# Query and key chunks of 128 different columns, and random features of head pairs as 32-row products in four row tiles

## The reference, cut to what matters

```python
qkv = (x @ W_qkv).reshape(b, n, 3, H, DH)            # H = 12 heads, DH = 16
q, k, v = (qkv[0], qkv[1], qkv[2])                   # after a transpose
def _phi(t, random_features):                        # M = 64 random features
    norm_sq = 0.5 * jnp.sum(t * t, axis=-1, keepdims=True)
    proj = jnp.einsum('bhnd,md->bhnm', t, random_features)
    return jnp.exp(proj - norm_sq) * (1.0 / math.sqrt(M))
q_p = _phi(q, random_features)
k_p = _phi(k, random_features)
kv = jnp.einsum('bhnm,bhnd->bhmd', k_p, v)
out = jnp.einsum('bhnm,bhmd->bhnd', q_p, kv)
normalizer = jnp.einsum('bhnm,bhm->bhn', q_p, jnp.sum(k_p, axis=2))[..., None]
out = out / (normalizer + 1e-06)
```

## Time and profile before

| what | value |
| --- | --- |
| median of 3 runs | 511.91 us (508.93 to 514.75) |
| span of the profiled execution | 511.0 us |
| TensorE busy | 424.5 us (83%), 2630 instructions |
| TensorE weight loads busy | 298.8 us (58%) |
| VectorE busy | 307.6 us (60%) |
| ScalarE busy | 227.5 us (45%) |
| GpSimd busy | 159.0 us (31%) |
| mean granted clock of TensorE | 0.883 of full speed |
| attention's features stage, first L750 to first L809 | 18.3, 17.2, 15.5 and 15.4 us in groups 0 to 3 |

### The profile page before, as it was taken

One profiled execution on the slowest core, in us unless ns is written; L12 is line 12 of the kernel. 1 busy time (PEld: TensorE's weight loads), 2 busy tenths in 40 slices (PEclk: granted clock), 3 DMA queues, 4 the chain that ended last, 5 costly groups with the idle time before them and its releaser, 6 DMA issues.

```text
span 511.0 us, 7813 instructions
## 1 busy us (share of the span) xinstructions
PE 424.5 (83%) x2630; PEld 298.8 (58%) x2630; DVE 307.6 (60%) x1180; ACT 227.5 (45%) x548; POOL 159.0 (31%) x168
## 2 busy tenths in 40 slices
PE   4992546599778989998798899799779888988997
PEld 2571333466474558665765685466647675666576
DVE  4561538453345778955369885844569895458222
ACT  2373335433435675344333753626245652652520
POOL 3106757201436552006265440005365410000000
PEclk9996669559985589999889999699799999999999
DMA  5559844659725332077234430086244310000000
GB/s 137 138 144 269 207 133 120 186 181 228 210 62 142 94 90 81 1 186 217 64 108 114 140 98 2 1 210 192 69 133 107 98 47 1 0 1 2 17 1 17
DMA packets 60022, 54.27 MB, mean 106 GB/s; under 512 B 44242, under 2 KB 52335, under 8 KB 59983
## 3 DMA queue, kind: packets, MB, share of 16 engines
q0 software_dynamic: 9216, 28.32, 19.6%
q1 hardware_dynamic: 50336, 25.42, 19.4%
q10 hardware_dynamic: 431, 0.03, 0.1%
HBM read 38.70 MB, written 15.06 MB: 105 GB/s over the span
## 4 chain that ended last, share of the span: by engine, by line
PE 64%; DVE 12%; ACT 8%; issue 6%; another core or an unknown queue 3%; POOL 3%; DMA 2%; ACTq 1%; DVEq 0%; POOLq 0%
PE bank L899 7%; PE bank L871 6%; PE bank L668 6%; PE bank L593 4%; PE bank L574 4%; PE bank L878 4%; PE bank L809 3%; PE bank L790 3%; PE bank L604 3%; POOL ring L519 3%; PE bank L794 2%; PE bank L825 2%; PE bank L750 2%; PE bank L552 2%
## 5 line engine op out<-in xcount | busy, mean ns | idle before, releaser
L519 POOL DMA_INDIRECT ring<-cells,cell x144 | 146.5, 1018 | 221.6 <-DVE cell L1334 100.0
L1356 DVE SCALAR_TENSOR_TENSOR bank<-ring,corner,bank 128x96 f32<-128x96 f32 x224 | 52.9, 312 | 26.1 <-ACT bank L1074 22.9
L668 PE MATMUL bank<-w_dcn,shared 128*128 128x192 f32 x192 | 44.8, 376 | 21.4 <-ACT shared L1083 13.2
L1198 ACT ACTIVATE hid<-bank,b_up 128x288 f32<-128x288 f32 x72 | 32.1, 497 | 63.6 <-PE bank L878 55.8
L871 PE MATMUL bank<-xfT,w_up 128*128 128x288 f32 x144 | 47.9, 458 | 5.8 <-ACT hid L1198 3.5
L668 PEld LDWEIGHTS bank<-w_dcn,shared 128*128 128x128 f32 x192 | 34.9, 212 | 30.3 <-ACT shared L1083 18.0
L899 PE MATMUL bank<-w_down,hid 128*128 128x192 f32 x288 | 52.1, 332 | 0.0
L899 PEld LDWEIGHTS bank<-w_down,hid 128*128 128x128 f32 x288 | 46.2, 190 | 4.6 <-issue 4.4
L871 PEld LDWEIGHTS bank<-xfT,w_up 128*128 128x128 f32 x144 | 27.0, 208 | 15.4 <-ACT hid L1198 5.7
L1074 ACT ACTIVATE bank<-ring,corner 128x96 f32<-128x96 f32 x112 | 31.4, 336 | 6.7 <-DMA ring<-cells,cell 5.5
L574 PE MATMUL bank<-xt,w_stem 48*96 48x384 f32 x96 | 32.6, 774 | 1.2 <-DVE h L1373 1.2
(11 more groups left out here) (182 smaller groups left out, 699.0 us busy)
## 6 DMA issues: line engine op xcount, KB each, us to landing
cells<-ring SPq DMA_DIRECT2D x16, 864.0 KB, 8.1
xs<-in_x_dram SPq DMA_DIRECT2D x28, 108.0 KB
ring<-cells,cell POOLq DMA_INDIRECT x144
w_down<-in_L_ffn_W_dram SPq DMA_DIRECT2D x3, 576.0 KB, 7.1
hid<-in_L_tok_dcn_w_dram SPq DMA_DIRECT2D x1, 1152.0 KB, 7.6
w_up<-in_L_ffn_W_dram SPq DMA_DIRECT2D x3, 384.0 KB, 3.8
out_dram<-y SPq DMA_DIRECT2D x8, 96.0 KB, 2.2
w_up_rest<-in_L_ffn_W_dram SPq DMA_DIRECT2D x6, 96.0 KB, 4.2
```

Of the source, the lines that this page charges most:

```text
L519: pool.indirect_dma_start(ring[:, ring_slot(k), j, :], None, table[0:HALF_CELLS, :] if k < EARLY else table, bass.IndirectOffsetOnAxis(ap= ...
L668: mm = pe.matmul(tokens_out(t), samp[:, n % 2, i, :], w_dcn[:, CHUNKS * (k % QUADS) + i, :], start=(k % QUADS == 0 and i == 0), stop=(k % ...
L1198: act.activation(hid[:, e % 2, f, :], up_bank(g, n)[:, 0:TOK], ACT.Gelu, bias=b_up[:, n:n + 1]).then_inc(gelu_done, 1)
L1356: ins = dve.scalar_tensor_tensor(acc[:, k % 3, :, j, :] if c == 3 else part_sum, ring[:, ring_slot(k), j, C1 * c:C1 * (c + 1)].rearrange(" ...
```

## The change

Query and key columns stand once: `w_qk` is [128, 3, 128], and a chunk is 128 different columns, which are eight heads. There are three chunks for queries and keys (`QK = 3`), one bank each; the values have three banks of their own. VectorE copies a whole chunk of 128 partitions to `qk[:, n]`, and ScalarE squares that copy, from SBUF to SBUF, into `qk[:, 3 + n]`. A pair of heads is 32 rows of a chunk (`quad`). Its features are the sum of two products of 32 rows each, one with the values against `w_feat[:, 0]` and one with the squares against `w_feat[:, 1]` (-0.5 under the mask). Four pairs in the four quarters of the rows go to four banks. The banks are now one tensor, so an exponential can read several: two query pairs (576 values in a partition) or four or two key pairs of one tile of tokens. There are nine exponentials a group instead of twelve, and the semaphores' counts follow (`EXPS = 9`). The random vectors are loaded eight times instead of four, and one of two copies of `w_qk` is gone.

The core of the diff:

```diff
-        w_qk = sb("w_qk", [128, 6, 2, 64])
-        w_qk_rest = sb("w_qk_rest", [128, 3, 2, 64])
+        w_qk = sb("w_qk", [128, QK, 128])
+        w_qk_rest = sb("w_qk_rest", [128, QK, 128])
...
-            for d in range(2):
-                sp.dma_start(w_qk[:, :, d, :], w["W_qkv"][0:WIDE, 0:2 * C2].rearrange("p (n c) -> p n c", c=64)).then_inc(ld_attn, 16)
+            sp.dma_start(w_qk[:, :, :], w["W_qkv"][0:WIDE, 0:2 * C2].rearrange("p (n c) -> p n c", c=128)).then_inc(ld_attn, 16)
...
-                    pool.wait_ge(exp_done, 12 * (g - 1) + 10)
+                    pool.wait_ge(exp_done, EXPS * (g - 1) + 7)
...
             def qkv(g, has_next):
                 pe.wait_ge(t2_evac, 3 * g + 1)
                 query_key(g, 0, has_next)
-                value(g, 0, 2)
                 query_key(g, 1, has_next)
-                value(g, 2, 3)
+                value(g, 0)
+                value(g, 1)
+                pe.wait_ge(t2_evac, 3 * (g + 1))
+                query_key_rest(0)
+                query_key_rest(1)
+                value_rest(0, 0)
+                value_rest(1, 1)
                 query_key(g, 2, has_next)
+                value(g, 2)
+                query_key_rest(2)
+                value_rest(2, 1)
+
+            def q_features(pairs, first):
+
+                for part in range(2):
+                    for p in pairs:
+                        r = p % 4
+                        mm = pe.matmul(ps[first + r][:, 0:TOK], w_feat[quad(r), part, :], qk[quad(r), QK * part + p // 4, :],
+                                       start=(part == 0), stop=(part == 1))
+                        if part == 1 and p % 2 == 1:
+                            mm.then_inc(feat_mm, 1)
+
+            def k_features(t, pairs, first):
+
+                t0, n = TILES[t]
+                for part in range(2):
+                    for p in pairs:
+                        r, c = (6 + p) % 4, (6 + p) // 4
+                        mm = pe.matmul(ps[first + r][0:n, 128 * t:128 * t + 128], qk[quad(r), QK * part + c, t0:t0 + n],
+                                       w_feat[quad(r), part, :], start=(part == 0), stop=(part == 1), skip_group_check=True)
+                mm.then_inc(feat_mm, 1)
 
             def features(g):
 
+                pe.wait_ge(q_copied, QK * g + 2)
+                pe.wait_ge(q_squared, QK * g + 1)
+                q_features((0, 1, 2, 3), 0)
+                pe.wait_ge(exp_done, EXPS * g + 2)
+                pe.wait_ge(q_copied, QK * (g + 1))
+                pe.wait_ge(q_squared, QK * (g + 1))
+                for t in range(3):
+                    k_features(t, (2, 3, 4, 5), 0)
                 pe.wait_ge(v_evac, 3 * (g + 1))
-                for u in range(12):
...
+                for t in range(3):
+                    k_features(t, (0, 1), 4)
+                q_features((4, 5), 4)
 
             def kv_sums(g):
-                pe.wait_ge(exp_done, 12 * g + 10)
...
             def squares(g):
-                for n in range(6):
-                    act.wait_ge(qk_mm, 6 * g + n + 1)
-                    act.activation(qk[64:128, n, :], ps[2 + n % 3][64:128, 0:TOK], ACT.Square).then_inc(q_squared, 1)
+                for n in range(QK):
+                    act.wait_ge(q_copied, QK * g + n + 1)
+                    act.activation(qk[:, QK + n, :], qk[:, n, :], ACT.Square).then_inc(q_squared, 1)
...
             def exps(g):
-                for u in range(12):
...
+                q_exps(g, 1, 0, 0)
+                q_exps(g, 2, 2, 2)
+                for t in range(3):
+                    k_exps(g, 5, t, 0, 2, 4)
+                for t in range(3):
+                    k_exps(g, 8, t, 6, 0, 2)
+                q_exps(g, 9, 4, 4)
...
-            for i in range(4):
+            for i in range(8):
                 act.dma_start(feat_nat[:, i, :], w["random_features"]).then_inc(ld_nat, 16)
...
             def q_copies(g, first, last):
                 for n in range(first, last):
-                    dve.wait_ge(qk_mm, 6 * g + n + 1)
-                    dve.tensor_copy(qk[0:64, n, :], ps[2 + n % 3][0:64, 0:TOK]).then_inc(q_copied, 1)
+                    dve.wait_ge(qk_mm, QK * g + n + 1)
+                    dve.tensor_copy(qk[:, n, :], ps[2 + n][:, 0:TOK]).then_inc(q_copied, 1)
```

More of the change, by code:

```diff
@@ L55 @@
 PAIRS = HEADS // 2
+QK = 2 * C2 // 128
+QUAD = 32
 VW = DH + 1
@@ L215, in build @@
         xs_second = flat[0:ROWS, 2 * HALF + C2:2 * HALF + C2 + CIN * STRIDE * SIDE].rearrange("p (r x) -> p r x", x=SIDE)
-        ps = [ctx.enter_context(nc.psum_tensor(f"bank{i}", [128, 512], F32)) for i in range(8)]
+        banks = ctx.enter_context(nc.psum_tensor("bank", [128, 8, 512], F32))
+        ps = [banks[:, i, :] for i in range(8)]
         ld_stem, ld_small, ld_dcn, ld_attn, ld_ffn = (sem(n) for n in ("ld_stem", "ld_small", "ld_dcn", "ld_attn", "ld_ffn"))
@@ L758, in value, with query_key @@
-            def value(g, first, last):
-                for t in range(first, last):
-                    t0, n = TILES[t]
-                    if t == 2:
-                        pe.wait_ge(v_evac, 3 * g + 1)
-                    pe.matmul(ps[t % 2][0:n, 0:C2], lnT[:, 0, t0:t0 + n], w_v[:, 0, :], start=True, stop=False)
-                for t in range(first, last):
-                    t0, n = TILES[t]
-                    pe.matmul(ps[t % 2][0:n, 0:C2], lnT[lower(t % 2), 1, t0:t0 + n], w_v[lower(t % 2), 1, :],
-                              start=False, stop=True).then_inc(v_mm, 1)
+            def query_key(g, n, has_next):
+                if n < 2 and has_next:
+                    pe.wait_ge(bn_evac, bn_done(g + 1, 12))
+                elif n == 2 and has_next:
+                    pe.wait_ge(idx_ready, 2 * g + 4)
+                elif n == 2:
+                    pe.wait_ge(y_added, 9 * (g - 1) + 5)
+                pe.matmul(ps[2 + n][:, 0:TOK], w_qk[:, n, :], lnT[:, 0, :], start=True, stop=False)
@@ new lines, in query_key_rest, with value @@
+            def query_key_rest(n):
+                pe.matmul(ps[2 + n][:, 0:TOK], w_qk_rest[lower(n % 2), n, :], lnT[lower(n % 2), 1, :],
+                          start=False, stop=True).then_inc(qk_mm, 1)
+            def value(g, t):
+                t0, n = TILES[t]
+                if t == 0 and later(g):
+                    pe.wait_ge(gelu_done, 18 * (g - 1) + 12)
+                    pe.wait_ge(y_added, 9 * (g - 1) + 1)
+                pe.matmul(ps[5 + t][0:n, 0:C2], lnT[:, 0, t0:t0 + n], w_v[:, 0, :], start=True, stop=False)
@@ L769, in qkv, with value_rest @@
+            def value_rest(t, i):
+                t0, n = TILES[t]
+                pe.matmul(ps[5 + t][0:n, 0:C2], lnT[lower(i), 1, t0:t0 + n], w_v[lower(i), 1, :],
+                          start=False, stop=True).then_inc(v_mm, 1)
             def qkv(g, has_next):
```

111 lines of the change are left out of this document (40 added, 71 removed).

## The result

The changed kernel takes 521.15 us (median of 4 runs, 516.72 to 529.05), the kernel before 512.87 (4 runs): ratio 1.0148, 95% interval 1.0077 to 1.022. I had forecast 498.5. It came out slower, and the stage that the forecast is about did get shorter where nothing disturbs it. The profiled execution took 517.89 us, span 516.1 (before 511.0); its mean granted clock is 0.848, that of before 0.883.

What follows compares the result with a forecast made beforehand. TensorE, with 64% of the chain of waits, was taken as the bound. Stages -15.8, start +2.4 and weights -0.3 sum to -13.7 us, 498.2 from the 511.91 median, stated as 498.5; 8-in-10 range 493 to 508.

Steps and rivals of the forecast that it cites:

- The stage: Attention, first query-key product to first key-value sum: group 3 from 15.5 to 12.1 us, all four groups -15.8 us.
- the extra idle time of the earlier trace in groups 0 and 1: Stages of groups 0 and 1: 2.8 and 1.7 us of idle time of unshown cause, which may go or stay.
- The two halves of the array: Features: two key pairs take 1.32 us and two query pairs 0.97, as long as four, with half the array idle.
- the table load behind the third square: ScalarE in group 3's stage: third copy and square done at 5.7 us, then table load of 1.28 to 7.0.
- the start: ScalarE's queue issues eight random-feature loads instead of four, delaying the first copy of the stem's pixels: +2.4 us.
- The gap: Ahead of the key features TensorE stands idle about 1.7 us, waiting for two exponentials on ScalarE.
- A: Features: 32-row tiles do not run side by side; 517 us, or 535 if products too are serial; chance 0.08.
- B: Features: sets of four tiles run at less than full pace, 0.7 us a group, 501 us; chance 0.12.
- C: Features: the array takes only two row tiles at once, +2.3 us a group, 507.5 us; chance 0.08.
- Rival E: Downstream, gathers landing no earlier or waiting feed-forward work take back half the gain, 505 us; chance 0.07.
- the term of nothing for all that lies behind the stage: Key-value sums and all behind them are the same instructions, so their change was counted as 0.
- rival D: Clock falls ahead of the sums, which take up to 1.7 times as long in groups 0 to 2: +8, 506 us; chance 0.1.

Runs made afterwards that it cites:

- small gathers: The changed kernel and the kernel before, each with gathered cells cut to 384 bytes: 482.15 and 485.21 us, one against the other 0.994.
- Keys first with eight loads: Changed kernel with key features ahead of query features and sums in banks 5 to 7: 474.86 us, 0.974 to the kernel before (488.67 us).
- filling: Changed kernel with four unneeded full 128-row products in TensorE's wait ahead of the key features: 482.60 us, 0.988 to the kernel before.

## Why the prediction was wrong

**The stage was right.** Group 3: 12.1 us forecast, 11.6 measured. On the faster kind the four undisturbed stages are 11.1, 12.1, 12.1 and 11.6 us where the kernel before has 15.5, 15.5, 15.5 and 15.4 (small gathers): 14.8 us, forecast 15.8. There the extra idle time of the earlier trace rows in groups 0 and 1 is absent, so it belongs to the slower kind. The two halves of the array, the table load behind the third square and the start (+2.4, measured +2.6) came as written. The gap was 2.35 us, not 1.7: TensorE was through 5.8 us into the stage, where I had 6.5, and the exponentials ended at 8.1 (forecast 8.2). I had let the key exponentials keep step tile by tile; they wait until a bank's products of all tiles are done, and that cost nothing. Rivals A, B and C are out: four row tiles run at the pace of one, for query and key sets. The 3.07x that the Trainium skill ("TensorE: Matmul & The Clock Gate", "Measured speedup vs the span model") gives for four row tiles, in a row for 512 columns, is not borne out by these fp32 products of 288 columns. Nor did the loads of 32 rows queue as feared under A: 0.110 us pays for four of them with their products. Rival E is not what happened: the time was lost in the attention itself.

**The step that failed** is the term of nothing for all that lies behind the stage. I costed the sums and attend at 0, because "the same instructions" stand there, and gave their slowing (rival D) a chance of 0.1 and +8 us. Measured, the sums took +12.8 us. Of these the half clock of groups 0 and 1 is 3.8 us each; the other 5.2, in groups 1 and 2, are results of TensorE that came late, which none of my rivals had and whose cause is open (below). The stage gave -8.3 for -15.8: the granted clock over the stages of groups 0 to 2 was 0.89, 0.83 and 0.89, and in group 0 the gap itself lasted 3.4 us. I had priced D for the sums alone, at up to 1.7 times their time; at half clock they took 1.95 times (7.75 us). Where one group falls and its neighbour does not, a fall costs 7.5 us, stage, sums and the way to the projection together. I also wrote that group 3, fed by other products, never fell; it fell in three of five profiles of the changed order on the slower kind. The gap I had seen, and priced as idle time of 1.7 us.

**What the gap explains.** The falls in group 3, and on the faster kind in every group: filled or made shorter by order, no fall in any. In time the two remedies do not agree. Keys first with eight loads gives 0.974 for 0.993, 9 us, of which 2.9 are its shorter stages (against filling) and not the clock; filling gives 0.988, 2.4 us, and the intervals of that pair overlap. The rest of the difference is not explained; the time at which the first attention starts alone varies from 110 to 117 us among the profiles of this kind. That 0.974 is also the forecast ratio is luck: it is another order of products, on another kind of chip.

**What stays open.** On the slower kind groups 0 to 2 fall even without it. There, results of TensorE arrive late although the clock is shown full. ScalarE takes the sums of group 0 of the kernel before on such a chip (start us, us, engine, line, what, idle before):

```profile
141.76 0.30 ACT L1178 ACTIVATE kv<-bank 64x153 f32<-64x153 f32 x1 [0.37 <-PE bank L809]
142.43 0.30 ACT L1178 ACTIVATE kv<-bank 64x153 f32<-64x153 f32 x1 [0.37 <-PE bank L809]
144.32 0.25 ACT L1178 ACTIVATE kv<-bank 64x102 f32<-64x102 f32 x1 [1.59 <-PE bank L809]
145.78 0.25 ACT L1178 ACTIVATE kv<-bank 64x102 f32<-64x102 f32 x1 [1.21 <-remote]
```

The sums come 0.67 us apart and then 1.89 and 1.46, with the granted clock shown at 1.00 until 146.1, and TensorE's rows of the sums ending at 143.7. The same pair is late in groups 1 and 2 and not in group 3, and in the two profiles of the kernel before on the faster kind nowhere, one of them with its gathers whole. In the changed kernel's first profile it is worse (start of ScalarE's copies in group 2, where the clock is shown at 1.00 throughout):

```profile
365.58 0.30 ACT L1213 ACTIVATE kv<-bank 64x153 f32<-64x153 f32 x1
367.05 0.30 ACT L1213 ACTIVATE kv<-bank 64x153 f32<-64x153 f32 x1 [1.17 <-PE bank L834]
368.53 0.30 ACT L1213 ACTIVATE kv<-bank 64x153 f32<-64x153 f32 x1 [1.18 <-PE bank L834]
369.97 0.58 ACT L1213 ACTIVATE kv<-bank 64x153 f32<-64x153 f32 x3 [1.15 <-PE bank L834]
```

An array already at half speed before the record says so would look like this. The Trainium skill ("TensorE: Matmul & The Clock Gate", Part 1, "Seeing it yourself") says that the records of this clock have been seen to be unreliable on trn2; these rows fit that, and do not prove it. Whether the gathers have a part in it (they run in groups 0 to 2 and not in 3) is open: the runs with moved or smaller gathers are all of the faster kind. Nor is it known what makes a chip one or the other.

## What to carry to other kernels

A shorter stage need not be shorter time if TensorE stands idle in it: give what lies behind the stage a price at half clock, and look for an order in which the engine waits less (here the larger half of the features first) before counting the gain. A fall cost about three times the gap here (7.5 us for 2.35), in one group of four on the faster kind. Compare variants on one chip, and a close call on chips of both kinds; here the sign changed between them. And look in the trace whether an edit made the gap that it was meant to make, before reading what followed.

## What the runs showed of the hardware

- Four 32-row tiles side by side take the time of one: 0.245 us for four fp32 passes of 288 columns, 0.110 for four key passes. The granted clock was 1.00 through both stretches (15.7 and 10.6 us).
- One 32-row tile alone, issued back to back for 36 us, fell to the 1.2 GHz level (mean granted clock 0.54), though the engine was never idle.
- A load of 64 rows on ScalarE's queue holds that engine 0.64 us (5.10 for eight); one load that repeats its source eight times holds it 0.69.
- The same program, the kernel before, had medians of 488.7 to 489.3 us in sets 1, 4 and 5 and of 508.2 to 513.0 in sets 2 and 3 and in the first measurement, sets 1 to 5 each on another chip. Its mean granted clock is 0.90 to 0.93 over the runs of the faster sets and 0.86 to 0.91 over those of the slower.
- With the granted clock shown at 1.00, ScalarE took the results of the sums (six passes of 0.11 us each) 0.67 us apart in the profiles of the kernel before on the faster kind, and up to 1.89 us apart on the slower.
